# Weigh a unit's first piece ahead of the third score product, and reorder SyncE's DMAs in a period

## The reference

```python
h = jnp.maximum(_layernorm(x, axis=-1), 0.0)
q = h @ Wq.T + bq
k = h @ Wk.T + bk
v = h @ Wv.T + bv
a = q @ k.T * scale + adj + adj
out = x + jax.nn.softmax(a, axis=-1) @ v
```

## Time and profile before

| | |
|---|---|
| median of 3 runs | 727.5 us (726.57 to 727.71) |
| profiled execution, own time | 730.97 us |
| its span | 729.2 us |
| TensorE matmul busy | 691.5 us, 95% of the span |
| VectorE busy | 598.0 us, 82% |
| ScalarE, GpSimd busy | 433.7 us and 432.0 us, 59% each |
| mean DMA rate | 221 GB/s |

### The profile page before, as it was taken

One profiled execution on the slowest core, in us unless ns is written; L12 is line 12 of the kernel. 1 busy time (PEld: TensorE's weight loads), 2 busy tenths in 40 slices (PEclk: granted clock), 3 DMA queues, 4 the chain that ended last, 5 costly groups with the idle time before them and its releaser, 6 DMA issues.

```text
span 729.2 us, 14700 instructions
## 1 busy us (share of the span) xinstructions
PE 691.5 (95%) x4799; PEld 472.2 (65%) x4799; DVE 598.0 (82%) x1282; ACT 433.7 (59%) x732; POOL 432.0 (59%) x436
## 2 busy tenths in 40 slices
PE   4589999899989899999999999999999999999988
PEld 4455554566757576666666666666666676666766
DVE  4889877879777788888797878797887978887996
ACT  3799663566565566574665656656656565656530
POOL 1789603556565656565565657565646566564667
PEclk7799999999999999999999999999999999999999
DMA  7298588898979899998989898989889898987473
GB/s 263 104 285 224 141 232 232 239 242 228 245 183 235 220 259 223 246 238 212 243 232 241 221 251 202 266 225 256 227 227 247 234 234 240 243 223 196 111 190 77
DMA packets 93244, 161.06 MB, mean 221 GB/s; under 512 B 20976, under 2 KB 41840, under 8 KB 93168
## 3 DMA queue, kind: packets, MB, share of 16 engines
q1 hardware_dynamic: 68432, 126.41, 65.7%
q10 hardware_dynamic: 24736, 33.72, 18.7%
HBM read 80.35 MB, written 8.39 MB: 122 GB/s over the span
## 4 chain that ended last, share of the span: by engine, by line
PE 64%; DVE 9%; DMA 8%; issue 6%; POOL 4%; ACTq 3%; SPq 3%; ACT 3%; DVEq 0%; POOLq 0%
PE bank L1443 35%; PE bank L1504 28%; DMA xT<-rows 4%; ACTq L789 3%; DMA xy<-in_x 3%; SPq L420 2%; POOL wT L625 2%; DVE rows L1128 1%; DVE stats L1046 1%; DVE rows L1101 1%; ACT wT L807 1%; DMA rows<-in_x 1%; DVE top L1137 1%; POOL a_op L602 1%; DVE row_max L1162 1%
## 5 line engine op out<-in xcount | busy, mean ns | idle before, releaser
L625 POOL TENSOR_TENSOR wT<-xT,wT 128x512 f16<-128x512 f32 x233 | 268.8, 1165 | 219.3 <-ACT wT L807 217.7
L1443 PE MATMUL bank<-v_sb,wT 128*128 128x256 f16 x2796 | 344.0, 273 | 7.2 <-POOL wT L625 4.2
L1504 PE MATMUL bank<-top,a_op 128*128 128x512 f16 x1344 | 330.8, 379 | 4.5 <-DVE chunk_max L1101 2.3
L1443 PEld LDWEIGHTS bank<-v_sb,wT 128*128 128x128 f16 x2796 | 272.4, 98 | 91.0 <-POOL wT L625 6.3
L1504 PEld LDWEIGHTS bank<-top,a_op 128*128 128x128 f16 x1344 | 130.8, 98 | 114.5 <-DVE chunk_max L1101 3.6
L778 ACT ACTIVATE rows<-rows,exp_bias,exp_scale 128x1024 f32<-128x1024 f32 x128 | 158.7, 1240 | 58.1 <-issue 31.3
L807 ACT CAST wT<-xT 128x512 f16<-128x512 f32 x233 | 137.3, 609 | 87.2 <-PE bank L1443 42.1
L1101 DVE CUSTOM_DVE_ANT_0 rows<-bank,rows 128x512 f32<-128x512 f32 x256 | 173.5, 680 | 10.7 <-PE bank L1504 2.3
L1128 DVE STREAM_TRANSPOSE rows<-rows 128x1024 f32<-128x1024 f32 x128 | 158.3, 1239 | 9.9 <-ACT rows L778 9.7
L1086 DVE SCALAR_TENSOR_TENSOR rows<-rows,adj_scale,bank 128x512 f32<-128x512 f32 x64 | 47.7, 745 | 48.0 <-PE bank L1504 48.0
L1079 DVE SCALAR_TENSOR_TENSOR rows<-rows,adj_scale,bank 128x512 f32<-128x512 f32 x64 | 47.6, 744 | 20.2 <-PE bank L1504 19.3
(11 more groups left out here) (115 smaller groups left out, 463.0 us busy)
## 6 DMA issues: line engine op xcount, KB each, us to landing
rows<-in_adj SPq DMA_DIRECT2D x128, 512.0 KB, 5.8
xT<-rows SPq DMA_DIRECT2D x488, 64.0 KB, 3.6
xT<-rows ACTq DMA_DIRECT2D x488, 64.0 KB, 4.1
rows<-in_x SPq DMA_DIRECT2D x8, 512.0 KB, 6.2
xy<-in_x SPq DMA_DIRECT2D x32, 128.0 KB, 5.7
g_scratch<-xT SPq DMA_DIRECT2D x16, 256.0 KB, 3.3
g_pair<-g_scratch SPq DMA_DIRECT2D x15, 256.0 KB, 7.2
out_y<-xy SPq DMA_DIRECT2D x30, 128.0 KB, 5.1
```

The costliest lines, as they stand in the source:

```text
L625: nc.gpsimd.tensor_tensor(split_piece(m, 1), exchanged(m), split_piece(m, 0), ALU.subtract).then_inc(split_lo, 1)
L1443: return nc.tensor.matmul(out_ap, stationary, moving, start=first, stop=last)
L1504: last = nc.tensor.matmul(ps[:], s, mv, start=first and k == 0, stop=k == 2, skip_group_check=True)
```

## The change

On TensorE the first piece of weighing of a period goes ahead of product 3 of the period before. In SyncE's period the store of the odd tile and the load of x go first, then `exchange_a`, then the first `refill`, then `load_g`, the second `refill` and the even tile's store. Nothing is added or removed.

```diff
@@ SyncE @@
             def period(n):
                 p, u = n // QUADS, n - EXP_LAG
+                if n % QUADS == 0 and p >= 3:
+                    store(2 * (p - 3) + 1)
+                if n % QUADS in (0, 1) and 2 <= p < PAIRS:
+                    load_xy(2 * p + n % QUADS)
+                if unit_in_range(u):
+                    exchange_a(u)
                 if unit_in_range(u - 1):
                     refill(u - 1, 0)
                 if n % QUADS == 0 and p + 1 < PAIRS:
                     load_g(p + 1)
-                if unit_in_range(u):
-                    exchange_a(u)
                 if unit_in_range(u - 1):
                     refill(u - 1, 1)
                 if n % QUADS == 3 and p >= 2:
                     store(2 * (p - 2))
-                if n % QUADS == 0 and p >= 3:
-                    store(2 * (p - 3) + 1)
-                if n % QUADS in (0, 1) and 2 <= p < PAIRS:
-                    load_xy(2 * p + n % QUADS)
@@ TensorE @@
                 if scoring:
                     product_1(n)
+                fill(n, 0)
                 if SETUP < n <= PERIODS:
                     product_3(n - 1)
-                fill(n, 0)
                 if scoring:
                     product_6(n)
                     product_2(n)
```

## The result

The change makes the kernel slower: 735.19 us median (731.62 to 741.24, 5 runs) against 727.71 (726.57 to 728.47, 5 runs). The ratio is 1.0093, 95% interval 1.0064 to 1.0123, so +7.5 us where +15 was forecast. The profiled execution took 732.83 us with a span of 731.1. Executions over 1.5% longer than the fastest of their kernel are left out of medians and ratios; there are two, 757.19 and 761.96 us, both of the kernel with the queries later still.

What follows compares the result with a forecast made beforehand. TensorE, busy all the time, sets the pace. Terms 15.6 + 3 + 0.5 + 1 - 5.1 = +15.0 us, 746.0 against the profiled 731.0; forecast median 742.5 us, range 726 to 757.

Steps and rivals of the forecast that it cites:

- The late queries: SyncE's load_g, behind the store's wait and exchange, makes GpSimd's low part late; TensorE idles 1.3 us 12 times: 15.6 us.
- It lands 7.5 us later, the median: SyncE's load_g in period 28, issued at 347.2, was to land at 354.7, by the old place's median landing time.
- a second row load adds 1.9 us: SyncE's queue: two row loads ahead of the even store in place of one make it take 6.1 us, not 4.2.
- The margin: TensorE's idle time ahead of the third period's second piece's low half: 0.9 to 1.7 us, taken as 1.3.
- The first rival: Wait for the store is short, GpSimd's slack covers late queries: 722 to 727 us; decided at landing about 353; chance 0.18.
- The signs of being wrong: Forecast wrong if first-period exchange_a still starts within 7 us of T(n), or query sums never wait for g_pair.
- Loads of x first: SyncE's earlier load of x removes ScalarE's waits and all of TensorE's steady idle time: -5.1 us, bounds 0 and 5.1.
- Piece 0 and product 3: TensorE's swap: piece 0 waits for finish, 3 us; later product 3 delays product 7 through VectorE's chain, 0.5 us.
- The shortened `row_max`: VectorE, pair's first period: started later, behind GpSimd, row_max falls from 0.90 to 0.22 us, so product 7 is not late.
- The tail: Last product 3 comes 1.31 us later, delaying VectorE's chain to TensorE's last pieces: 1 us, bounds 0 and 1.3.

Runs made afterwards that it cites:

- the queries later still: Dose: kernel with only SyncE's order changed, load_g moved from behind the first period's exchange to ahead of the second's; 748.55 us, ratio 1.0288.
- SyncE's part alone: Kernel before with only SyncE's new order (store and load of x first, exchange ahead of row load and load_g), TensorE's order as before; 728.59 us, ratio 1.0000.
- g_behind: Kernel before with one move: load_g behind exchange_a in place of ahead of it; 727.88 us, ratio 1.0002.
- the version with no wait for `g_pair` and 1.9 us for x: TensorE's order as before; SyncE does load_g, exchange_a, store and load of x, then both row loads; 728.07 us, ratio 1.0005.
- the kernel that differs only in period 64: Kernel before with piece 0 ahead of product 3 only in period 64; 729.3 us against 728.31, ratio 1.0008.
- the one with second and third periods changed: Kernel before with piece 0 ahead of product 3 only in a pair's second and third periods; 727.61 us, ratio 0.9992.
- TensorE's part alone: Kernel before with only piece 0 ahead of product 3, SyncE's order as before; 735.51 us against 727.92, ratio 1.0093.
- first periods alone: Kernel before with piece 0 ahead of product 3 only in a pair's first period, tail excepted; 736.23 us, ratio 1.0096.
- `finish` moved ahead: Piece 0 ahead of product 3 only in a pair's first period, and finish ahead of row_bias on VectorE; 731.21 us, ratio 1.005 against 1.0096.
- the dose of 0.65 us: Kernel with only first periods changed, and there product 3 also behind product 6, another 0.65 us later; 741.47 us, ratio 1.0178.
- the queries first: The whole change, but load_g at the very start of SyncE's period, ahead of the store and load of x; 733.62 us, ratio 1.0075.
- 7 slots: The whole change with a ring of 7 slots for x and the output in place of 6; 734.19 us, ratio 1.0075.
- TensorE's part and `finish` first: Only TensorE's new order, all periods, with finish ahead of row_bias on VectorE in a pair's third and fourth period; 733.99 us, ratio 1.008.

## Why the prediction was half wrong

The side was right, and so were most of the mechanisms, but the forecast was twice the result: one term was far too large, one gain was not there, and two terms together were too small.

**The late queries: 15.6 us forecast, 0.7 found. This step failed.** Up to `load_g` the mechanism went as written, at smaller sizes: the store is waited for, the exchange starts 8.7 us after T(n) in the median (7.9 to 10.3; 10.0 forecast) and `load_g` is issued at 15.1 (13.9 to 16.4; 15.4 forecast). The error is the sentence "It lands 7.5 us later, the median". Those twelve loads had two row loads in the 4 us ahead of them; in the new place, behind the exchange and one row load, they land in 5.2. The prediction had taken from the earlier trace rows that a second row load adds 1.9 us, and used it for the store, but not for `load_g`, which loses one. The queries are there 19.8 us after T(n) in the median, not 22.9. The margin was 1.3 us, so 2.3 us less of landing time is everything. GpSimd's timeline in the changed kernel shows where it went:

```profile
347.41 1.16 POOL L625 TENSOR_TENSOR wT<-xT,wT 128x512 f16<-128x512 f32 x1 [2.91 <-ACT wT L807]
348.65 0.46 POOL L592 TENSOR_TENSOR comb<-g_pair 128x128 f32<-128x128 f32 x1
...
350.55 3.38 POOL L625 TENSOR_TENSOR wT<-xT,wT 128x512 f16<-128x512 f32 x3
```

The sums start at 348.65: `load_g`, issued 5.3 us before, landed just as GpSimd came free. In other pairs GpSimd waits up to 3.2 us, and its second piece's low part then ends up to 5.0 us after the third period's start, against the 4.8 that TensorE wants: at the edge, in three of 12 pairs. They are the three in which the queries landed 21.4 us or more after T(n). The first rival put the deciding point at 353 in period 28's terms, 21.2 us after T(28), and there it is. The signs of being wrong did not catch this: `exchange_a` starts over 7 us late and the sums do wait for `g_pair`, as forecast; what is missing is what that wait was to cause, TensorE's brackets of 1 to 2 us.

The dose shows that the rest of the chain was right. With `load_g` issued at some 17 and landing near 23 TensorE idles 24.1 us by starts in a profiled execution that ran 4.5 us above its median, and the median rises by 20 us over SyncE's part alone. `g_behind` shows the shorter landing time with TensorE's order and the load of x untouched; whether the place behind the exchange or the missing row loads made it shorter, it cannot tell.

**Loads of x first: -5.1 us forecast, nothing found.** The waits of ScalarE and the idle times of the earlier trace rows did go. But SyncE's part alone has a ratio of 1.0000, and the version with no wait for `g_pair` and 1.9 us for x has 1.0005. Those idle times seem to have been more those of one execution, 3.5 us above its median: in the kernel that differs only in period 64 they are 2.1 us by starts, in the one with second and third periods changed 0.2, and in `g_behind`, whose profiled execution lay 4.2 us above its median, 4.5. Reading a possible gain of 5.1 us off one execution was a mistake that its own distance to the median pointed at. How large they are in a median run was not measured.

**Piece 0 and product 3: 3.5 us forecast, about 6.5 found** (7.5 less 1.0 for the tail). Piece 0 was to wait for `finish` in first periods, 3 us in all. In the changed kernel it is 5.5 us by starts, and 3.2 of them stand in fourth periods, which the forecast did not count, though the bracket at 244.07 in the earlier trace rows is one; how much of either is new cannot be read off the kernel before, whose own 2.3 us are those of an execution 3.5 us above its median. With TensorE's part alone it is 2.8, all in first periods. The shortened `row_max` was right. VectorE's timeline of period 28, to be held against the earlier trace rows:

```profile
331.65 0.69 DVE L1101 CUSTOM_DVE_ANT_0 rows<-bank,rows 128x512 f32<-128x512 f32 x1 [1.14 <-PE bank L1504]
...
332.91 0.22 DVE L1162 SCALAR_TENSOR_TENSOR row_max<-tile_max,exp_scale,r_row 128x1 f32<-128x1 f32 x1 [0.29 <-DVE tile_max L1158]
...
333.24 0.74 DVE L1086 SCALAR_TENSOR_TENSOR rows<-rows,adj_scale,bank 128x512 f32<-128x512 f32 x1
```

`finish_12` starts 2.80 us after T(28) (2.84 forecast), `row_max` is at 0.22, and `scores_12` ends 5.13 after T(28), in time for product 7 at 5.21. Product 4 waits instead, 0.3 us in that period. Missing from the forecast was what else waits for the bias: the first exponential, whose wait rose from 14.8 to 26.5 us. With SyncE's old order TensorE also idles ahead of GpSimd's low part in fourth periods, 1.6 us with all periods changed and 3.8 with first periods alone; that the late exponential is the reason is likely, not shown. `finish` moved ahead takes away half of the loss and the dose of 0.65 us adds 5.2 us: both the output bank and the bias are at their edge.

**The tail: 1 us forecast, 1.0 found in the trace.** VectorE's idle time ahead of the last product 3, 0.35 us in the earlier trace rows, is now

```profile
688.26 0.69 DVE L1101 CUSTOM_DVE_ANT_0 rows<-bank,rows 128x512 f32<-128x512 f32 x1 [2.23 <-PE bank L1504]
```

and the end follows 55.3 us after the start of period 63 in place of 54.3.

What stays open: the changed kernel's runs scatter from 731.6 to 741.2 us, and those with the queries first or 7 slots from 731.4 to 737.2. The queries at the edge would explain the slowest of them, but a run of 739.9 us stands among those with TensorE's part and `finish` first, where the queries are early; no profile of such a run was taken.

## What to carry to other kernels

When a transfer is moved past others, take its time to land from transfers with the same loads just ahead of them, not from the median of the old place: here 2.3 us of landing time decided 15 us. An engine that orders its work by hand has slack that differs by period: the same swap was free in two periods of four and cost the whole 7 us in the one where a longer chain (`finish` and `bias`) hung on it, and a test of each kind of period alone finds that at once. And before counting a profile's idle times as what can be won, hold the profiled execution against the median.

## What the runs showed of the hardware

The landing time of the same 256 KB load of `g_pair` went with the number of 512 KB row loads that SyncE had issued in the 4 us ahead of it. In all 16 kernels of this case the 12 loads from 160 to 690 us have the same number: with two row loads (12 kernels) a kernel's median is 6.0 to 8.0 us, with one (the changed kernel, SyncE's part alone, 7 slots) 4.4 to 5.2, with none (`g_behind`) 3.5. The loads with one or none all stand behind the exchange's eight DMAs as well and the others do not, so the step from two to one is not separated from that place; between one and none the place is the same. The bytes moved are the same, and the mean DMA rate over the span was 220 and 221 GB/s.

A 128x1 instruction on VectorE with two inputs in SBUF took up to 1.2 us when it met a GpSimd instruction. In the changed kernel, where it starts when GpSimd has mostly finished, its times by source are these.

```profile
L1162 DVE SCALAR_TENSOR_TENSOR row_max<-tile_max,exp_scale,r_row x32: 219/219/874, 84.8 to 690.5; 128x1 f32<-128x1 f32 x32
```

Of the 14 first ones of a pair in periods 8 to 60, 12 took over 0.4 us before and 2 do now, and each of these 14 long ones ended within 0.02 us of the end of a GpSimd instruction, which was running when it started or, once, started 0.04 us later. That agrees with the lock on a shared pair of ports that the Trainium skill describes ("SBUF — State Buffer", SBUF: two separate sides); here a later start made the chain shorter.
